# Second cross-attention of a six-layer block: a symmetric product computed in three quarters and mirrored, started earlier, with the routed additions spread over the step

## The reference

```python
# third layer, what each row gets of its four experts
routed = jnp.einsum('etd,te->td', y, combine)
...
# fourth layer: x + _L1_xattn_ref(_layernorm(x), ctx_1024, ctx_1024)
def _L1_xattn_ref(qm, km, vm):
    scale = 1.0 / jnp.sqrt(jnp.asarray(qm.shape[-1], dtype=qm.dtype))
    qkm = jnp.einsum('bqd,bkd->bqk', qm, km) * scale
    out = jnp.einsum('bqk,bkd->bqd', qkm, vm)
    return jax.nn.softmax(out, axis=-1)
```

## Time and profile before

| | us |
|---|---|
| median of 3 runs (2391.7 to 2401.5) | 2396.54 |
| the profiled execution | 2406.51 |
| its span | 2404.7 |
| the fourth layer, from SP's first load to DVE's last update | 1577.5 to 1759.9 of the span |
| that layer's share | 182.3 |

### The profile page before, as it was taken

How to read it: one execution, slowest core, us unless ns; L and a number is a source line. 1 busy time by engine, 2 the same in 40 slices (tenths; PEclk the granted TensorE clock), 3 DMA queues, 4 the chain that set the end, 5 groups by cost and what they waited for, 6 DMA issues and landing times. The chain is left out here.

```text
span 2404.7 us, 57551 instructions
## 1 busy us (share of the span) xinstructions
PE 2142.6 (89%) x19514; PEld 1596.2 (66%) x19527; DVE 1492.1 (62%) x4179; ACT 1099.3 (46%) x2377; POOL 982.8 (41%) x1105
## 2 busy tenths in 40 slices
PE   7999999999899989998999999969978888477773
PEld 5888888888699976565666666646667787233331
DVE  5777777777666663982333333357757776577772
ACT  4666666666544533382222222223335555335442
POOL 3444444444200012444666666521124333036455
PEclk9999999999888989999999999989989999689996
DMA  4110110011000021131222222255500000000002
GB/s 133 32 30 29 38 31 29 29 29 47 2 11 11 9 65 50 44 158 40 85 87 83 87 86 84 78 186 201 199 6 10 7 9 8 35 1 1 0 0 70
DMA packets 120510, 128.80 MB, mean 54 GB/s; under 512 B 77537, under 2 KB 95074, under 8 KB 119138
## 3 DMA queue, kind: packets, MB, share of 16 engines
q1 hardware_dynamic: 105570, 89.23, 12.0%
q0 software_dynamic: 13824, 37.77, 5.0%
q10 hardware_dynamic: 1024, 0.61, 0.1%
HBM read 96.11 MB, written 27.26 MB: 51 GB/s over the span
## 5 line engine op out<-in xcount | busy, mean ns | idle before, releaser
L542 ACT ACTIVATE xa_prob<-xa_neg_s,xa_neg_max 128x256 f32<-128x256 f32 x512 | 224.5, 499 | 143.0 <-DVE xa_neg_max L420 142.9
L1896 PE MATMUL ex_ps_h<-moew_w,ex_xT 128*128 x576 | 274.8, 600 | 4.0 <-issue 1.9
L1944 DVE COPY ex_xT<-ex_ps_x 128x256 f32<-128x256 f32 x144 | 61.2, 425 | 248.2 <-PE ex_ps_x L1903 120.2
L420 DVE CUSTOM_DVE_ANT_0 xa_neg_s<-xa_ps_s,xa_mask 128x256 f32<-128x256 f32 x512 | 191.5, 421 | 33.9 <-PE xa_ps_s L607 19.6
L1873 POOL DMA_INDIRECT ex_xg<-xn_rows,moe_in_row x144 | 140.1, 973 | 111.4 <-issue 62.0
L636 PEld LDWEIGHTS xa_ps_o<-xa_v,xa_probT 128*64 128x64 f32 x4096 | 141.0, 138 | 48.2 <-issue 42.7
L549 ACT ACTIVATE xa_probT<-xa_ps_s 128x512 f32<-128x512 f32 x256 | 152.1, 594 | 41.8 <-PE xa_ps_s L618 40.8
L636 PE MATMUL xa_ps_o<-xa_v,xa_probT 128*64 128x34 f32 x4096 | 169.9, 227 | 0.2 <-ACT xa_probT L549 0.2
L1878 POOL DMA_INDIRECT expert_outs<-ex_y,moe_out_row x144 | 142.6, 990 | 60.0 <-issue 38.4
L1929 ACT ACTIVATE ex_act_g<-ex_ps_h 128x256 f32<-128x256 f32 x144 | 55.3, 384 | 242.9 <-PE ex_ps_h L1896 138.9
L618 PE MATMUL xa_ps_s<-g_ident,xa_prob 128*128 128x128 f32 x1024 | 162.9, 282 | 2.9 <-ACT xa_prob L542 2.7
(11 more groups left out here) (314 smaller groups left out, 5030.1 us busy)
## 6 DMA issues: line engine op xcount, KB each, us to landing
xa_ctxT<-in_ctxT_dram SPq DMA_DIRECT2D x32, 512.0 KB, 3.6
xb_ctx_rows<-in_ctx_rows_dram SPq DMA_DIRECT2D x32, 512.0 KB, 3.7
xb_expert_y<-expert_outs SPq DMA_DIRECT2D x32, 512.0 KB, 4.5
...
xn_rows<-rs_xn SPq DMA_DIRECT2D x8, 512.0 KB, 2.9
moew_xw<-in_moe_w_dram SPq DMA_DIRECT2D x8, 512.0 KB, 20.7
...
```

The lines of the kernel that those rows point to most:

```text
L420: ins = nc.vector.tensor_tensor_reduce(neg_s[:, u % 2, g, :], ps_s[j][:, g * S:(g + 1) * S], mask[:, b, :], -1.0, 3e38, ALU.add, ALU.min, ...
L542: ins = nc.scalar.activation(prob[:, u % 2, i, :], neg_s[:, u % 2, i, :], ACT.Exp, bias=neg_max[:, u % 2, i:i + 1], scale=-1.0)
L1896: mm = nc.tensor.matmul(ps_h[1 - par][:, :], xT[:, 1 - par, k, :], c.w1[:, own, k, :], start=(k == 0), stop=(k == KC - 1))
```

## The change

- PE computes, for each batch, the output blocks (0,0) and (0,1) in one call of 128 x 256 and the block (1,1) in one of 128 x 128, for each half of the context rows. The block (1,0) comes from a transpose of (0,1) (`mirror`), which PE makes from the scaled copy into PSUM, and which ACT copies back.
- PE forms the Gram matrices of tile s in step s (before: of tile s-3), ahead of the transposes of tile s-3. `gram` holds four tiles instead of two.
- ACT copies each batch's Gram blocks in two pieces, one batch ahead of the exponential and one behind it, then the mirrored block of tile s-2, then the transposed rows (`xT`) of tile s-3, which DVE copied before.
- DVE's four additions are spread: one ahead of the maximum, two behind it, one between reciprocal and update; the reciprocal and the update now stand ahead of the statistics.
- SP loads four tiles of context first, then waits for the experts' stores (the wait that ended the experts' phase on POOL), then alternates. The experts' result buffer `y` and its semaphores now outlive their phase.

```diff
-        y = ph.sb("y", [P, 4, E])
+        y, stored = c.y, c.y_stored
-        stored = [ph.sem(f"stored{i}") for i in range(4)]
...
-            for q in range(4):
-                pool.wait_ge(stored[q], 16 * (NS // 4))
...
+        GR = 4
-        gram = ph.sb("gram", [P, 2, 2, KC, E])
+        gram = ph.sb("gram", [P, 4, 2, KC, E])
...
+            for s in range(4):
+                sp.dma_start(ctx_rows[:, s, :, :], d["ctx_rows"][s, :, :, :]).then_inc(ctx_loaded[s], 16)
+            for q in range(4):
+                sp.wait_ge(c.y_stored[q], 16 * (NS // 4))
...
             def step(s, q):
                 if live(s):
-                    wait(sp, gram_done, 2 * (s - 3))
-                    sp.dma_start(ctx_rows[:, q, :, :], d["ctx_rows"][s, :, :, :]).then_inc(ctx_loaded[q], 16)
                     wait(sp, added, TOP * (s - 3))
                     sp.dma_start(expert_y[:, q, :, :], picked[s, :, :, :]).then_inc(gathered[q], 16)
-            tile_steps(sp, step, lag=0, turn=4, peel=8)
+                if live(s + 4):
+                    wait(sp, gram_done, 2 * (s + 1))
+                    sp.dma_start(ctx_rows[:, q, :, :], d["ctx_rows"][s + 4, :, :, :]).then_inc(ctx_loaded[q], 16)
...
+                sp_, tp, op, oq = q % 2, 1 - q % 2, q % 2, q
+                if live(s):
+                    pe.wait_ge(ctx_loaded[q], (s - q) * 4 + 16)
+                    for b in range(2):
+                        wait(pe, gram_ready, GR * (s - 2) + GR // 2 * (b + 1))
+                        for g in range(KC):
+                            for k in range(2):
+                                mm = nc.tensor.matmul(ps_g[sp_][b][:, g * (E + P):(g + 1) * E],
+                                                      ctx_rows[:, q, 2 * b + k, g * P:(g + 1) * P],
+                                                      ctx_rows[:, q, 2 * b + k, g * P:E], start=(k == 0), stop=(k == 1))
+                        mm.then_inc(gram_done, 1)
+                h = s - 2
+                if live(h):
+                    pe.wait_ge(gram_ready, GR * h + GR)
+                    wait(pe, xT_ready, h - 1)
+                    for b in range(2):
+                        mm = nc.tensor.transpose(ps_x[sp_][:, E + b * P:E + (b + 1) * P],
+                                                 gram[:, (q - 2) % 4, b, 0, P:E], c.ident[:, :])
+                    mm.then_inc(mirror_done, 1)
                 if live(t):
                     pe.wait_ge(ln.xn_ready, t + 1)
                     wait(pe, xT_ready, t - 1)
+                    pe.wait_ge(mirror_ready, t + 1)
...
-                    pe.wait_ge(ctx_loaded[tq], (t - tq) * 4 + 16)
...
-                    pe.wait_ge(gram_ready, 2 * o + 2)
+                    pe.wait_ge(mirror_ready, o + 1)
...
+                r = s - 1
+
+                def gram_out(b):
+                    act.wait_ge(gram_done, 2 * r + b + 1)
+                    wait(act, o_done, r - 3)
+                    nc.scalar.activation(gram[:, (q - 1) % 4, b, 0, :], ps_g[par][b][:, 0:E], ACT.Copy,
+                                         scale=E ** -0.5).then_inc(gram_ready, 1)
+                    nc.scalar.activation(gram[:, (q - 1) % 4, b, 1, P:E], ps_g[par][b][:, E + P:2 * E], ACT.Copy,
+                                         scale=E ** -0.5).then_inc(gram_ready, 1)
+
+                if live(r):
+                    gram_out(0)
                 if live(o):
                     act.wait_ge(max_ready, o + 1)
                     wait(act, x_updated, o - 1)
                     nc.scalar.activation(ex[:, par, :], ps_o[par][:, 0:E], ACT.Exp,
                                          bias=neg_max[:, par:par + 1],
                                          accum_out=total[:, par:par + 1]).then_inc(exp_ready, 1)
+                if live(r):
+                    gram_out(1)
+                if live(m + 1):
+                    act.wait_ge(mirror_done, m + 2)
+                    nc.scalar.activation(gram[:, (q - 2) % 4, :, 1, 0:P],
+                                         ps_x[1 - par][:, E:2 * E].rearrange("p (b t) -> p b t", b=2), ACT.Copy)\
+                        .then_inc(mirror_ready, 1)
                 if live(m):
-                    for b in range(2):
-                        act.wait_ge(gram_done, 2 * m + b + 1)
-                        wait(act, o_done, m - 1)
-                        nc.scalar.activation(gram[:, par, b, :, :].rearrange("p k e -> p (k e)"),
-                                             ps_g[par][b][:, :], ACT.Copy, scale=E ** -0.5).then_inc(gram_ready, 1)
+                    act.wait_ge(xT_done, m + 1)
+                    wait(act, o_done, m - 1)
+                    nc.scalar.activation(xT[:, par, :, :], ps_x[par][:, 0:E].rearrange("p (k t) -> p k t", k=KC),
+                                         ACT.Copy).then_inc(xT_ready, 1)
...
+                def add(k):
+                    wait(dve, added, TOP * l + k)
+                    nc.vector.scalar_tensor_tensor(X[:, l, :], expert_y[:, (q - 2) % 4, k, :],
+                                                   c.weight[:, l, k:k + 1], X[:, l, :],
+                                                   ALU.mult, ALU.add).then_inc(added, 1)
                 if live(t):
                     ln.normalise(dve, nc, t, 1 - par, xT_done)
+                if live(l):
+                    dve.wait_ge(gathered[(q - 2) % 4], (l - (q - 2) % 4) * 4 + 16)
+                    add(0)
                 if live(o):
...
                 if live(l):
-                    dve.wait_ge(gathered[(q - 2) % 4], (l - (q - 2) % 4) * 4 + 16)
-                    for k in range(TOP):
...
-                if live(t):
-                    dve.wait_ge(xT_done, t + 1)
-                    wait(dve, o_done, t - 1)
-                    nc.vector.tensor_copy(xT[:, 1 - par, :, :], ps_x[1 - par][:, 0:E].rearrange("p (k t) -> p k t", k=KC))\
-                        .then_inc(xT_ready, 1)
+                    add(1)
+                    add(2)
+                if live(o):
+                    dve.wait_ge(exp_ready, o + 1)
+                    nc.vector.reciprocal(rz[:, 1 - par:2 - par], total[:, 1 - par:2 - par]).then_inc(rz_ready, 1)
+                if live(l):
+                    add(3)
+                if live(o):
+                    dve.wait_ge(rz_ready, o + 1)
+                    nc.vector.scalar_tensor_tensor(X[:, o, :], ex[:, 1 - par, :], rz[:, 1 - par:2 - par], X[:, o, :],
+                                                   ALU.mult, ALU.add).then_inc(x_updated, 1)
                 if live(l):
                     wait_apart(dve, added, TOP * l + TOP, c.passed_dve)
                     ln.statistics(dve, nc, l, par)
-                if live(o):
...
```

30 lines of the change are left out of this document (11 added, 19 removed).

## The result

The changed kernel takes 2382.72 us (median of 6 runs, 2380.88 to 2387.67), the kernel before in the same comparison 2391.64 (6 runs, 2388.05 to 2401.5). By the medians that is 8.9 us or 0.37%; forecast were 9.4 us. The ratio over all fast runs is 0.9951, 95% interval 0.9932 to 0.9970, so the gain is real and lies between 7 and 16 us; by the bound of 0.5% it counts as no change. The profiled execution took 2384.92 us with a span of 2383.1. Up to the experts' last store it was 10.4 us ahead of the profile of before (1558.48 and 1568.91), a stretch in which the change moves nothing but a buffer, so the two traces are compared from the layer's start and not by their spans.

A forecast was written before the change was run, and what follows sets the result against it. DVE with POOL was taken to bound the loop, PE the straight-line steps. Loop 7.0, seam and fill 0, steps 32 to 34 0.6 and tail 1.8 sum to 9.4 us: median 2387.1 us, range 2376 to 2398.

The forecast's parts named there:

- What bounds the kernel: DVE with POOL bounds the 24 loop steps at 5.31 us, PE the eight or so straight-line steps at 4.86.
- The loop: 24 steps of the layer's loop: each falls from 5.31 to 5.02 us, a gain of 7.0 us.
- the leg over POOL: From the statistics' second half on DVE over POOL to the next normalisation: taken as 1.35 us, bounded by 1.21 and 1.63.
- the new circle: DVE's closed chain in a loop step, normalisation to next normalisation through POOL's answer, in the changed order: 5.02 us.
- The exponential in time: In a loop step ACT's exponential sum is ready 0.26 us before DVE's reciprocal needs it, so the reciprocal doesn't wait.
- Seam and fill: Experts' phase's end to step 8's normalisation: layer begins 1.0 us earlier, first addition 9.1 us after start; together gain 0.
- DVE can't use it: gain 0: Fill: PE's head start of four Gram tiles is real, but brings DVE nothing.
- Steps 32 to 34: Two straight-line steps behind the loop: 9.12 us instead of 9.73, gain 0.6 us.
- The tail: Last normalisation to the layer's end: 9.7 us, the middle of 7.95 and 11.50, gain 1.8 us.
- The short circle: Rival: loop step 4.56 us, as chained waits shrink and POOL answers in 1.21; median 2376.1 us; chance 0.15.
- The whole seam: Rival: the idle time between experts' phase and layer goes, layer begins up to 6.7 us earlier; 2380.4 us; chance 0.09.
- The clock: Rival: PE's clock falls to 1.2 GHz in a third of the loop steps; median 2415 us; chance 0.06.

The follow-up runs named there:

- e3: Changed kernel with all four Gram blocks computed by PE and no mirror: loop step 4.987 us, layer 177.47 us, ratio 0.9974 to the kernel before.
- e13: Kernel before with only DVE's order changed, next tile's first two additions behind the statistics; four Gram blocks: loop step 4.858 us, ratio 0.9956.
- e1: Kernel before with only the copy of xT moved from DVE to ACT: loop step 5.250 us, ratio 0.9984 to the kernel before.
- e4: Changed kernel with reciprocal and update put back behind the statistics on DVE: loop step 4.982 us, ratio 0.9939 to the kernel before.
- e5: Changed kernel with SP loading context rows and expert rows in turn from the start: fill 35.12 us, ratio 0.9944 to the kernel before.
- e7: Changed kernel with six memory fills on POOL between its last store and the experts' phase's end: the hold after POOL is through was 7.09 us.
- e9: Changed kernel with the next tile's first two additions, reciprocal and update moved behind the statistics' second half on DVE: loop step 4.277 us, ratio 0.9864.

## Why the prediction was right, and where it was not

**What bounds the kernel.** Right for the loop, and shown by e3 and e13: with all four blocks the loop is as fast as with three (4.987 and 4.985), and with another order on DVE it is faster with four (4.858).

**The loop, forecast 7.0 us, measured 7.75.** The step was 4.985 for 5.02; the leg over POOL is 1.32 on the mean for 1.35. That the longer legs go away when DVE has nothing to do beside POOL was right and worth 0.15 us a step, 3.7 of the 7.75; only that of the loop's turn stays 0.2 longer than the rest. It wasn't priced so: 1.35 was set near the shortest legs of before, and the bound of 1.63 was too low for them (1.72). The forecast came out because the new circle was written down link by link with the chained waits in it. When I worked by taking one instruction's time off the old circle, in e1 and e4, I was out by 6 to 9 us.

**The exponential in time.** Right: no idle time ahead of the reciprocal in the loop, so ACT ate nothing. Only in the tail it waits 0.63.

**Seam and fill, forecast together 0, measured −1.05.** The seam gave 1.71 for 1.0: POOL's last wait for a store ended at 1570.4, 1.5 us after 1568.91. In the fill three terms were off. The first addition came 10.61 us after the start for 9.1: three further loads of context cost 1.9 us each ((10.61 − 4.86) / 3), not 1.4; in the other traces with this order of loads it is 1.6 to 2.2. From first addition to first normalisation were 3.85 for 4.11, and the five steps behind took 22.00 for 21.6. "DVE can't use it: gain 0", said of PE's head start, was wrong. Before, DVE waited in the fill for PE's first product:

```profile
1597.01 0.42 DVE L2072 TENSOR_REDUCE xb_neg_max<-xb_ps_o 128x1 f32<-128x256 f32 x1 [1.57 <-PE xb_ps_o L2036]
```

In after it doesn't, and where the head start is smaller it waits again, 2.97 us in e5. The five steps took 24.73 us before (1586.51 to 1611.24) and 22.00 after. The sum had this gain in its five short steps without naming it; what came out near 0 is the head start's gain against the later first addition.

**Steps 32 to 34.** 0.71 for 0.6.

**The tail, forecast 1.8, measured 2.67.** The mis-sized term is the share of the 3.55 us Gram tile that goes: 75% and not half, where the middle had been taken for want of a nearer row.

**Sum.** 7.75 + 0.71 + 2.67 + 1.71 − 2.76 = 10.1 us between the two traces, 8.9 by the medians. Loop, tail, seam and steps 32 to 34 gave 2.4 us more than forecast, the fill lost 1.7 more, so part of the agreement with 9.4 is luck. And the whole program's time, known to some 4 us, can't tell 9.4 from 10.1; only the parts of the traces test the sum.

**The rivals.** The short circle: 4.985, not 4.56; the chained wait stays 0.62 in the loop with other work beside it. The whole seam: 6.9 of 8.6 us stay, fixed, as e7 shows. The clock: 1.00 in the loops of after and of e9, in the latter with PE busy without a pause. In the last 19 us of the layer in after it was 0.73, with PE busy for 9.03.
